# Per-token attention in score blocks of four tokens instead of eight, with its stages moved in the loop

## Chip, cores and metric

One core of a Trainium2 chip runs the whole program. The metric is the device time of one execution in microseconds (us). The kernel before takes 1196.86 us, the median of 3 runs (1196.32 to 1197.43).

## What is computed

The input is 8192 tokens of 256 features, in fp32 (4 sequences of 2048). A normalized copy passes a pre-norm transformer block whose attention runs inside each token, over its 16 heads; then a mixture of two chosen experts per sequence is added. The part that the change touches, in the reference:

```python
fq = jax.nn.elu(q) + 1.0
fk = jax.nn.elu(k) + 1.0
kv = jnp.einsum('bhnd,bhne->bnde', fk, v)
qkv = jnp.einsum('bhnd,bnde->bhne', fq, kv)
k_sum = fk.sum(axis=1)
qk = jnp.einsum('bhnd,bnd->bhn', fq, k_sum)
attn = qkv / (qk[..., None] + 1e-06)
```

The kernel uses the equivalent form per token n: the score of head h against head g is fq[h,n]·fk[g,n], the output of head h is the sum over g of score times v[g,n], and a column of ones beside v gives the denominator. The rest of the block (projections, an MLP of 1024 with exact gelu, layer norms, the experts) is the same before and after.

## The kernel before, in words

**Tiles and stages.** The tokens are cut into 16 tiles of 512. Each engine walks the same list of stages (`walk`, L134); `LAG` (L44) says how many iterations behind the newest tile a stage works, so one iteration of the loop (FULL, L46; HEAD, L48, at the start of a sequence) holds stages of up to six tiles. The list is written out by hand. Each engine issues its part of each stage in this order and waits on semaphores whose target values `walk` counts with the table `INC` (L70). An iteration has three sections here: the M stages (MLP of one tile, mixed with the attention of the tile behind it), the features and projections (X, VT, D2, A2, experts F1 and F3), and the ending (B0, H, FX, F2).

**Attention.** A tile's features q and k go through a DRAM scratch (`qk_dram`, stores L349 in stage D2, loads L372 in K0 and K1, 8 DMAs each), so that the 16 features of a head stand on 16 partitions, in four row groups (quarters j of the tile, 32 partitions apart). v goes the same way (`v_dram`, loads L361 in VL, 8 DMAs, then transposes in VT into `vb`). `scores(r)` (L913) takes 8 tokens times 16 heads as one 128 by 128 block: K is 16 rows, so four such matmuls, one for each quarter, can run in four row tiles of the array, each into its own bank of `ps`. A tile has 4 rounds of 4 blocks by 4 quarters, 16 matmuls a round; fp32 makes each matmul two records of the profile with a weight load each, 32 a round. Of a 128 by 128 block only the entries within a token count, one in eight; `masked(r)` (L675) multiplies by a 0/1 mask on VectorE, four banks of 512 columns a round, into `am` (two buffers). `weighted(r)` (L924) multiplies `am` (K 128) by v and ones (32 columns), four column tiles, into bank `pw[0]`, again 32 records a round; ScalarE copies it to `ot` (L532). After round 2 and round 4 SyncE stores half of `ot` to `nd_dram` (L377) and reads it back token by token (three loads, L382), in stages M2 and M4; VectorE divides in N0 and N (`divided`, L712).

**Stages M1 to M4 on TensorE** (L968 to L987), where `up` is one of the 8 up projections of the MLP (6 matmuls of 512 columns, L959) and `down` one of its 8 down projections (12 matmuls of 256 columns, L944):

- M1: up(0), up(1), scores(1), weighted(0), down(0)
- M2: up(2), scores(2), down(1), up(3), weighted(1), down(2)
- M3: up(4), scores(3), down(3), up(5), weighted(2), down(4)
- M4: up(6), down(5), up(7), weighted(3), down(6)

Before down(m) TensorE waits for VectorE's rest(m) (L694), which follows two gelus of ScalarE (L525, L526). scores(0) is B0, at the end of the iteration before, ahead of H: transposes of the second norm's output, from which ScalarE and VectorE make `hT` (L513, L710) that up(0) reads. F2 transposes the expert sum, adds it (L834) and stores the output (L400).

**SyncE's order** in an iteration: input load (L), x2 store (XS), 8 loads of v (VL), 8 of q and k for the first half (K0, after M1), nd store and 3 loads (M2), 8 loads (K1), nd store and 3 loads (M4), x2 load (XL), feature stores (D2), output store (F2). Each waits for its semaphores with all later DMAs queued behind it.

## Time and profile before

| | |
|---|---|
| median of 3 runs | 1196.86 us |
| profiled execution, its own time | 1194.7 us |
| its span in the trace | 1192.9 us |
| TensorE matmul busy | 1048.4 us (88%) |
| VectorE busy | 729.8 us (61%) |
| ScalarE busy | 499.5 us (42%) |
| GpSimd busy | 178.5 us (15%) |
| mean DMA share of queue 1 | 36.0% |
| granted TensorE clock, mean | 0.928 of full |

Busy is the union of an engine's instructions. The profiled execution took 1.8 us more than its span, and lies 2.2 us under the median. A granted clock of 1.0 is 2.4 GHz, of 0.5 is 1.2 GHz. M stages with attention of a tile run in iterations that begin (first up projection) at 117.5, 178.7, 240.4, 302.0, 363.6, 436.6, 500.6, 564.5, 630.3, 702.9, 766.9, 830.8, 896.1, 967.8 and 1032.5 us; one more tile's attention runs without an MLP between 61 and 90 us. The iterations from 436.6 on are preceded by F2. In section 3 of the page queue q1 carries SyncE's DMAs.

### The profile page before, as it was taken

The numbers are of one execution on the slowest core, as the hardware profiler recorded it, in microseconds if no ns is written. First come the engines' busy times: TensorE is split into PE (matmuls) and PEld (weight loads), VectorE is DVE, ScalarE is ACT, GpSimd is POOL, SyncE is SP. The second block draws the span as 40 slices with busy tenths as digits, with TensorE's granted clock in tenths as the row PEclk, the third lists the DMA queues.
The fourth block names the chain that finished last, engine by engine and source line by source line (L and its number), as shares of the span: only waits on it lengthen the run. The fifth ranks groups of instructions, "written<-read, shape, count | busy, mean of one in ns | idle before, by whom it ended". The sixth has DMA issues, their size and how long they took to land.

```text
span 1192.9 us, 23418 instructions
## 1 busy us (share of the span) xinstructions
PE 1048.4 (88%) x8136; PEld 779.5 (65%) x8136; DVE 729.8 (61%) x1692; ACT 499.5 (42%) x771; POOL 178.5 (15%) x113
## 2 busy tenths in 40 slices
PE   5767989898998899999999899999999896987856
PEld 3445858676777668585867667685868565665623
DVE  2286566666666666766666675766667674645333
ACT  2313444544353444445453545444453433332322
POOL 1021020211111111102021112112020111111000
PEclk9757989999898899999999999999999899998969
DMA  5635343434242443443544344433445434121023
GB/s 178 149 76 122 78 121 79 124 75 123 71 114 77 113 109 95 119 102 93 135 101 118 107 111 106 119 93 105 115 101 138 108 84 97 37 65 68 14 75 106
DMA packets 255833, 119.93 MB, mean 101 GB/s; under 512 B 225168, under 2 KB 241808, under 8 KB 255504
## 3 DMA queue, kind: packets, MB, share of 16 engines
q1 hardware_dynamic: 249104, 108.47, 36.0%
q10 hardware_dynamic: 6656, 10.50, 2.4%
q8 instruction: 45, 0.74, 0.3%
q14 instruction: 28, 0.23, 0.1%
HBM read 60.20 MB, written 58.72 MB: 100 GB/s over the span
## 4 chain that ended last, share of the span: by engine, by line
PE 72%; issue 11%; DVE 9%; POOL 2%; DMA 2%; ACT 2%; DVEq 0%; SPq 0%; ACTq 0%; POOLq 0%
PE pw L959 16%; PE pj L944 15%; PE ps L920 10%; PE ps L902 7%; PE pw L930 5%; PE pw L870 5%; PE pj L870 4%; PE pw L902 3%; DVE am L680 3%; PE ps L1001 3%; PE ps L858 2%; DVE hT L710 1%; POOL x_sb L447 1%; PE pw L910 1%; ACT hidden L526 1%
## 5 line engine op out<-in xcount | busy, mean ns | idle before, releaser
L959 PE MATMUL pw<-hT,w_fc 128*128 128x512 f32 x768 | 212.1, 417 | 30.4 <-DVE hT L710 29.7
L944 PE MATMUL pj<-w_pj,hidden 128*128 128x256 f32 x1536 | 214.1, 289 | 1.4 <-DVE hidden L694 1.4
L694 DVE TENSOR_TENSOR hidden<-xhT,hidden 128x512 fp32r<-128x512 f32 x128 | 88.6, 692 | 201.1 <-ACT hidden L526 201.1
L944 PEld LDWEIGHTS pj<-w_pj,hidden 128*128 128x128 f32 x1536 | 192.3, 189 | 22.5 <-issue 14.9
L525 ACT ACTIVATE xhT<-pw,col 128x512 f32<-128x512 f32 x128 | 88.1, 688 | 279.9 <-PE pw L959 279.3
L959 PEld LDWEIGHTS pw<-hT,w_fc 128*128 128x128 f32 x768 | 144.5, 199 | 66.1 <-DVE hT L710 31.7
L680 DVE TENSOR_TENSOR am<-ps,mask 128x512 f32<-128x512 f32 x256 | 158.9, 684 | 17.6 <-PE ps L920 17.5
L920 PE MATMUL ps<-kq 16*128 16x128 f32 x2048 | 146.9, 438 | 16.0 <-DVE am L680 9.2
L920 PEld LDWEIGHTS ps<-kq 16*128 16x128 f32 x2048 | 128.5, 329 | 42.3 <-issue 33.3
L902 PE MATMUL ps<-xhT,w_qkv 128*128 128x512 f32 x256 | 120.6, 627 | 2.5 <-ACT xhT L478 2.5
L532 ACT ACTIVATE ot<-pw,den_eps 128x512 f32<-128x512 f32 x64 | 81.8, 1278 | 49.6 <-PE pw L930 49.6
L719 DVE RECIPROCAL nd<-nd 128x256 f32<-128x256 f32 x32 | 56.0, 1749 | 60.2 <-DMA nd<-scratch_nd 60.2
L902 PEld LDWEIGHTS ps<-xhT,w_qkv 128*128 128x128 f32 x256 | 51.0, 205 | 61.6 <-issue 58.4
L526 ACT ACTIVATE hidden<-pw,col 128x512 fp32r<-128x512 f32 x128 | 87.2, 681 | 0.0
L672 DVE SCALAR_TENSOR_TENSOR fqk<-am 128x512 f32<-128x512 f32 x64 | 43.2, 690 | 59.6 <-ACT am L502 59.6
L444 POOL TENSOR_TENSOR x<-x,row 128x1024 f32<-128x1024 f32 x16 | 37.7, 2354 | 271.5 <-DVE x_sb L755 271.5
L1001 PE MATMUL ps<-w_o,hT 128*128 128x256 f32 x384 | 57.0, 308 | 21.2 <-DVE hT L730 21.2
L930 PE MATMUL pw<-am,vb 128*32 128x128 f32 x2048 | 73.0, 286 | 1.9 <-ACT ot L532 1.4
L930 PEld LDWEIGHTS pw<-am,vb 128*32 128x32 f32 x2048 | 54.6, 113 | 23.2 <-issue 16.4
L1001 PEld LDWEIGHTS ps<-w_o,hT 128*128 128x128 f32 x384 | 51.0, 203 | 28.7 <-DVE hT L730 21.6
L870 PE MATMUL pw<-zT,w_e 128*128 (+1 forms) x128 | 59.9, 612 | 7.2 <-DMA b_e<-in_eb 7.2
L902 PE MATMUL pw<-xhT,w_qkv 128*128 128x512 f32 x128 | 57.5, 592 | 0.0
(109 smaller groups left out, 1165.0 us busy)
## 6 DMA issues: line engine op xcount, KB each, us to landing
scratch_nd<-ot SPq DMA_DIRECT2D x32, 512.0 KB, 4.1
nd<-scratch_nd SPq DMA_DIRECT2D x96, 128.0 KB, 2.6
x_sb<-in_x SPq DMA_DIRECT2D x16, 512.0 KB, 4.6
scratch_v<-feat_v ACTq DMA_DIRECT2D x16, 512.0 KB, 2.8
scratch_q<-fqk SPq DMA_DIRECT2D x32, 256.0 KB, 2.7
scratch_k<-fqk SPq DMA_DIRECT2D x32, 256.0 KB, 3.0
vd<-scratch_v SPq DMA_DIRECT2D x128, 64.0 KB, 2.7
kq<-scratch_q SPq DMA_DIRECT2D x128, 64.0 KB, 2.5
```

The source lines that it names most:

```text
L525: nc.scalar.activation(gelub[:, m % 2], pw[n], ACT.Gelu, bias=b_fc[:, m:m + 1])
L526: nc.scalar.activation(hidden[:, m % SLOTS, 0], pw[n], ACT.Gelu, bias=b_fc[:, m:m + 1]).then_inc(S[f"pw_free{n}"], 1)
L532: nc.scalar.activation(dst[:, r // 2, RG * (r % 2):RG * (r % 2 + 1)], src, ACT.Identity, bias=den_eps[:, :]).then_inc(S["pw_free0"], 1)
L680: last = nc.vector.tensor_tensor(am[:, r % 2, j].rearrange("p (g n) -> p g n", n=P), ps[:, j].rearrange("p (g n) -> p g n", n=P), mask[:, ...
L694: nc.vector.tensor_tensor(hidden[:, m % SLOTS, 1], gelub[:, u], hidden[:, m % SLOTS, 0].bitcast(f32), ALU.subtract).then_inc(S["rest_ready ...
L870: last = nc.tensor.matmul(bank, w[:, c, P * m:P * (m + 1)], zT[:, p.t % RING, c], start=(c == 0), stop=(c == NC - 1))
L902: last = nc.tensor.matmul(bank, w_qkv[:, j // NC, c, P * (j % NC):P * (j % NC + 1)], xhT[:, c], start=(c == 0), stop=(c == NC - 1))
L920: last = nc.tensor.matmul(ps[:, j, P * g:P * (g + 1)], kd[rows, r // 2, at_g], qd[rows, r // 2, at_g], start=True, stop=True)
L930: last = nc.tensor.matmul(pw[0][32 * j:32 * j + 32, P * g:P * (g + 1)], vb[:, GG * j + RG * r + g], am[:, r % 2, j, P * g:P * (g + 1)], st ...
L944: last = nc.tensor.matmul(pj[u][:, D * s:D * (s + 1)], hidden[:, m % SLOTS, a, lo:lo + P], w_pj[:, b, m], start=(m == 0 and n == 0 and s = ...
L959: last = nc.tensor.matmul(pw[bank], w_fc[:, b, c, P * m:P * (m + 1)], hT[:, a, c], start=(n == 0), stop=(n == len(order) - 1))
L1001: last = nc.tensor.matmul(sa[u][:, D * s:D * (s + 1)], attnT[:, a, c, lo:lo + P], w_o[:, b, c], start=(c == 0 and n == 0), stop=(c == NC - ...
```

## The change

Blocks are of 4 tokens by 16 heads, 64 by 64. Two of them (v, which splits each half of a quarter once more) stand in the upper and lower 64 columns of the array, so `scores` issues eight tile positions in turn (4 row groups, 2 column groups) and fills all four banks of `ps` in one call for half of the tile. There are now two calls, scores(0) in B0 and scores(1) in M2, each of 64 matmuls (128 records), and two of `weighted` with 64 matmuls (128 records; K 64, 32 columns of weights, 64 columns moved; 2 row groups by 4 column groups), which write banks sa[0] and sa[1] (banks 0 and 1 of `ps`) instead of pw[0]. VectorE masks 4 banks a call, 8 instructions a tile instead of 16, and `am` is one buffer. ScalarE still copies 4 banks a tile into `ot`, two after each `weighted`. With `pw[0]` free, the up projections alternate between pw[0] and pw[1]. TensorE's order becomes:

- M1: up(0), up(1), weighted(0), down(0)
- M2: up(2), scores(1), down(1), up(3), down(2)
- M3: up(4), down(3), weighted(1), up(5), down(4)
- M4: up(6), down(5), up(7), down(6)

In the stage list K0 stands before M1 and K1 behind M2, N0 stands before M4 instead of behind it, and H before B0. Scratch q and k are stored in runs of 32 tokens (128 bytes) instead of 64; v is loaded with 16 DMAs instead of 8, in the same short runs; M2 and M4 wait for sa instead of pw[0] before the nd store.

```diff
-TB = 4
+TB = 2
 TA = 2 * TB
...
+BLOCK = TA * H
+KG = HALF // (2 * TA)
+ROUNDS = 4
...
-FULL = ["L", "XS", "VL", "M1", "K0", "J2", "Y", "M2", "DS", "M3", "Z", "D1", "K1", "M4", "N0", "XL", "X", "J7", "JA", "YB", "E", "VT", "N", "D2", "A2",
-        "F1", "R", "F3", "F4", "SA", "B0", "H", "FX", "F2"]
+FULL = ["L", "XS", "VL", "K0", "M1", "J2", "Y", "M2", "K1", "DS", "M3", "Z", "D1", "N0", "M4", "XL", "X", "J7", "JA", "YB", "E", "VT", "N", "D2", "A2",
+        "F1", "R", "F3", "F4", "SA", "H", "B0", "FX", "F2"]
...
-    "kq_in0": {"K0": 32 * NQ}, "kq_in1": {"K1": 32 * NQ}, "v_in": {"VL": 32 * NQ},
+    "kq_in0": {"K0": 32 * NQ}, "kq_in1": {"K1": 32 * NQ}, "v_in": {"VL": 64 * NQ},
...
-        am = sb("am", [P, 2, NQ, 512])
+        am = sb("am", [P, NQ, 512])
...
-        qk_dram = [nc.dram_tensor(f"scratch_{n}", (2, 2 * NQ, D, HALF), f32, kind="Internal").ap() for n in "qk"]
+        qk_dram = [nc.dram_tensor(f"scratch_{n}", (2, 4 * NQ, D, HALF // 2), f32, kind="Internal").ap() for n in "qk"]
...
                         for b in range(2):
-                            sp.dma_start(vd[2 * j + b::2 * NQ].rearrange("p (h t) -> p h t", h=H), src[j, b]).then_inc(S["v_in"], 16)
+                            for v in range(2):
+                                sp.dma_start(vd[2 * j + b::2 * NQ].rearrange("p (v h t) -> p v h t", v=2, h=H)[:, v],
+                                             src[j, b, v]).then_inc(S["v_in"], 16)
...
-                    wait("pw_free0", at("pw_free0", 1))
+                    for u in range(2):
+                        wait(f"sa_free{u}", at(f"sa_free{u}"))
                     sp.dma_start(nd_dram.rearrange("j e h t -> (j e) h t")[:, :, part], ot[:, :, part]).then_inc(S["nd_out"], 16)
...
+                        if "B" in parts and r % 2 == 0 and u == int(r == 0):
+                            dst = ot[:, :, :].rearrange("p h (b v a k) -> p b v k h a", b=2, v=2, k=KG)
+                            for v in range(2):
+                                wait(f"sa_full{v}", at(f"sa_full{v}", 1))
+                                src = sa[v].rearrange("p (k h a) -> p k h a", k=KG, h=H)
+                                nc.scalar.activation(dst[:, r // 2, v], src, ACT.Identity,
+                                                     bias=den_eps[:, :]).then_inc(S[f"sa_free{v}"], 1)
...
-                def scores(r):
+                def scores(b):
 
                     wait("sc_free", at("sc_free"))
-                    for g in range(RG):
-                        at_g = slice(RG * (r % 2) + g, P * HG, HG)
-                        for j in range(NQ):
-                            rows = slice(32 * j, 32 * j + HD)
-                            last = nc.tensor.matmul(ps[:, j, P * g:P * (g + 1)], kd[rows, r // 2, at_g], qd[rows, r // 2, at_g],
-                                                    start=True, stop=True)
+                    for k in range(KG):
+                        for v in range(2):
+                            for j in range(NQ):
+                                rows = slice(32 * j, 32 * j + HD)
+                                cols = slice(BLOCK * KG * v + k, BLOCK * KG * (v + 1), KG)
+                                last = nc.tensor.matmul(ps[BLOCK * v:BLOCK * (v + 1), j, BLOCK * k:BLOCK * (k + 1)],
+                                                        kd[rows, b, cols], qd[rows, b, cols], start=True, stop=True)
                     last.then_inc(S["sc_full"], 1)
 
-                def weighted(r):
+                def weighted(b):
 
                     wait("sc_free", at("sc_free"))
...
+                    for k in range(KG):
+                        for v in range(2):
+                            rows = slice(BLOCK * v, BLOCK * (v + 1))
+                            cols = slice(BLOCK * k, BLOCK * (k + 1))
+                            for j in range(NQ):
+                                last = nc.tensor.matmul(sa[v][32 * j:32 * j + 32, cols], vb[rows, KG * (2 * j + b) + k],
+                                                        am[rows, j, cols], start=True, stop=True)
```

## Rows read from the trace of the kernel before

**Rows 1.** The page: span, TensorE's busy time, the chain that ended last by line

```profile
span 1192.9 us, 23418 instructions
...
PE 1048.4 (88%) x8136; PEld 779.5 (65%) x8136; DVE 729.8 (61%) x1692; ACT 499.5 (42%) x771; POOL 178.5 (15%) x113
...
PE pw L959 16%; PE pj L944 15%; PE ps L920 10%; PE ps L902 7%; PE pw L930 5%; PE pw L870 5%; PE pj L870 4%; PE pw L902 3%; DVE am L680 3%; PE ps L1001 3%; PE ps L858 2%; DVE hT L710 1%; POOL x_sb L447 1%; PE pw L910 1%; ACT hidden L526 1%
```

**Rows 2.** Groups by line, shapes apart: busy us, mean ns of one, idle before

```profile
L920 PE MATMUL ps<-kq 16*128 16x128 f32 x2048 | 146.9, 438 | 16.0 <-DVE am L680 9.2 <-DVE x L740 6.8
...
L680 DVE TENSOR_TENSOR am<-ps,mask 128x512 f32<-128x512 f32 x256 | 158.9, 684 | 17.6 <-PE ps L920 17.5
...
L532 ACT ACTIVATE ot<-pw,den_eps 128x512 f32<-128x512 f32 x64 | 81.8, 1278 | 49.6 <-PE pw L930 49.6
...
L719 DVE RECIPROCAL nd<-nd 128x256 f32<-128x256 f32 x32 | 56.0, 1749 | 60.2 <-DMA nd<-scratch_nd 60.2
```

**Rows 3.** TensorE in time, inner iteration at 564: start, us, idle before

```profile
564.52 4.60 PE L959 MATMUL pw<-hT,w_fc 128*128 128x512 f32 x12 [2.16 <-DVE hT L710]
...
569.05 2.29 PE L920 MATMUL ps<-kq 16*128 16x128 f32 x32
...
571.28 1.08 PE L930 MATMUL pw<-am,vb 128*32 128x128 f32 x32
...
572.29 1.67 PE L944 MATMUL pj<-w_pj,hidden 128*128 128x256 f32 x12
...
597.99 1.70 PE L944 MATMUL pj<-w_pj,hidden 128*128 128x256 f32 x12
```

**Rows 4.** Weight loads in time, the first 0.3 us of the weighted sums at 571

```profile
571.28 0.38 PEld L930 LDWEIGHTS pw<-am,vb 128*32 128x32 f32 x16 [0.22 <-issue]
```

**Rows 5.** TensorE and VectorE in time, end of that iteration

```profile
623.65 2.29 PE L920 MATMUL ps<-kq 16*128 16x128 f32 x32
...
625.87 1.09 PE L858 MATMUL pw<-ident,hn 128*128 128x128 f32 x8
...
628.41 1.28 DVE L710 TENSOR_TENSOR hT<-pw,hT 128x512 fp32r<-128x512 f32 x2
...
629.61 1.28 DVE L834 TENSOR_TENSOR out_sb<-pj,out_sb 128x512 f32<-128x512 f32 x2
...
630.32 1.89 PE L959 MATMUL pw<-hT,w_fc 128*128 128x512 f32 x7 [2.49 <-DVE hT L710]
```

**Rows 6.** SyncE's queue in time, same iteration (start, us of issuing)

```profile
565.58 0.38 SPq L400 DMA_DIRECT2D out<-out_sb  x1
...
568.75 5.29 SPq L361 DMA_DIRECT2D vd<-scratch_v  x8
...
574.77 1.92 SPq L372 DMA_DIRECT2D kq<-scratch_q  x4
...
583.29 0.57 SPq L377 DMA_DIRECT2D scratch_nd<-ot  x1
...
587.46 1.50 SPq L382 DMA_DIRECT2D nd<-scratch_nd  x3
```

**Rows 7.** The page, DMA issues: KB each, us to landing

```profile
nd<-scratch_nd SPq DMA_DIRECT2D x96, 128.0 KB, 2.6
```

**Rows 8.** Windows around one score burst each: busy, granted clock, DMA share

```profile
70.80:73.10 2.30, 2.27 (x36) 2.05 (x39) 0.00 (x0) 0.00 (x0) 0.00 (x0) 0.50 0.00 0
...
569.00:571.30 2.30, 2.30 (x37) 2.03 (x36) 1.16 (x2) 1.27 (x2) 0.00 (x0) 1.00 0.91 301
```

**Rows 9.** TensorE in time, end of an iteration without expert stages

```profile
165.56 3.44 PE L1001 MATMUL ps<-w_o,hT 128*128 128x256 f32 x24
...
178.69 4.80 PE L959 MATMUL pw<-hT,w_fc 128*128 128x512 f32 x12 [1.80 <-DVE hT L710]
```

**Rows 10.** TensorE in time, last iteration with attention

```profile
1032.53 3.07 PE L959 MATMUL pw<-hT,w_fc 128*128 128x512 f32 x12 [1.91 <-DVE hT L710]
...
1079.31 5.03 PE L1001 MATMUL ps<-w_o,hT 128*128 128x256 f32 x24 [10.97 <-DVE hT L730]
```

More of the change, by code:

```diff
@@ L26 @@
 HALF = QT // 2
-TB = 4
+TB = 2
 TA = 2 * TB
-GG = QT // TA
-RG = 4
-HG = GG // 2
-ROUNDS = GG // RG
+BLOCK = TA * H
+KG = HALF // (2 * TA)
+ROUNDS = 4
 TERMS = ((0, 0), (1, 0), (0, 1))
@@ L515, in run @@
                     parts, r = of_round(p.stage)
-                    if "C" in parts:
-                        for m in (2 * r, 2 * r + 1):
-                            n = int(m != 1)
-                            more = int(r > 0 and m % 2)
-                            wait(f"pw_full{n}", at(f"pw_full{n}", more + 1))
+                    for u in range(2):
+                        if "C" in parts:
+                            m = 2 * r + u
+                            wait(f"pw_full{u}", at(f"pw_full{u}", 1))
@@ L949, in up @@
                 def up(m):
-                    bank = int(m != 1)
-                    wait(f"pw_free{bank}", at(f"pw_free{bank}", int(m > 1 and m % 2)))
+                    bank = m % 2
+                    wait(f"pw_free{bank}", at(f"pw_free{bank}"))
                     if m == 0:
                         wait("h_round", at("h_round"))
-                        wait("pw_free0", at("pw_free0"))
+                        for c in range(NC):
+                            wait(f"pw_free{c}", at(f"pw_free{c}"))
                     order = [(a, b, c) for a, cb in ((0, (0, 1)), (1, (0,))) for c in range(NC) for b in cb]
```

110 lines of the change are left out of this document (48 added, 62 removed), and 2 rows, old and new, of the table INC.

## The prediction

> **What bounds the kernel now.** I read the page first: TensorE is busy for 1048 of 1193 us, and the chain that ended last runs mainly over its lines, 10% of it scores and 5% weighted sums [rows 1]. Then the groups: a score record takes part in 146.9 us of work, and the masks cost VectorE 158.9 us, but VectorE isn't the bound, so halving its 256 masks is worth nothing by itself beyond what TensorE waits for [rows 2]. The timeline of one iteration shows TensorE without a gap through the M stages; what it loses lies at the ending, where up(0) waits 2.2 to 2.5 us for hT, which VectorE makes behind four masks [rows 3, 5]. Last I read SyncE's queue, which this change loads further [rows 6]: there the price of the change hides.
>
> A word on names: E is the end of the experts' F3 (623.65, where B0 begins), T0 the start of up(0), and F2 end the end of the output addition (L834). S is one of the new score calls and W one of the new weighted calls, each half a tile, each 128 records.
>
> **Price of S.** Now 32 records go by in 2.23 us (569.05 to 571.28), eight groups of four row tiles, 0.28 us a group [rows 3]. This pace is the same at a granted clock of 0.50 and of 1.00 [rows 8], so it is set by how four row tiles read 128 columns, not by the array's clock. Lower end: a group of eight tiles with half the columns takes half the time, 16 x 0.14 = 2.2 us. Upper end: a group takes as long as now, since it reads as many columns in all, 16 x 0.28 = 4.5 us. I take 2.4, near the lower end, because a row group and its columns are what seems to set the pace.
>
> **Price of W.** Now 32 records take 1.01 us, 31.6 ns each, with 128 columns moved in four column tiles [rows 3]. Lower end: half the columns, eight tiles, 16 x 0.063 = 1.0 us. Upper end: the pace per record stays, 128 x 31.6 ns = 4.0 us. Of the 32 weight loads at 571.28 the first 16 start within 0.38 us [rows 4], less than 24 ns apart, and about 18 when the last one's own duration is taken off. At 18 ns a record, W = 2.3 us, which I take; S at that pace would be 2.3 as well.
>
> A page of the Trainium skill, "TensorE: Matmul & The Clock Gate" (Part 1), gives a floor of about 25 ns from one matmul's start to the next, however few columns. By it S = W = 3.2 us. The loads in rows 4 start closer than that, but a short burst is no proof for 128 in a row, so it stands among the rivals.
>
> **M stages, TensorE alone.** Before, T0 to down(6) is 33.5 us in the iteration at 564 [rows 3], of which 3 score rounds and 4 weighted rounds are 3 x 2.23 + 4 x 1.01 = 10.7, and 1.5 come from up(0) and up(1) at a low clock (4.6 us against 3.1, [rows 3, 10]). The rest is 21.3. After: 21.3 + S + 2W = 28.3, plus some 0.5 in M3, where gelu(5) stands behind two copies into ot of 1.28 us each [rows 2] and down(5) comes too early for it.
>
> **Ending.** Before: B0, then H (0.93 us to the next start), F2 as much, then the wait; T0 is at E + 6.7 [rows 5]. After: H first, so ScalarE and VectorE make hT (1.1 + 1.3 us) while S runs, and that wait is gone: T0 at E + 1.9 + S = E + 4.3. VectorE's masks come behind hT (2.48 us) and F2's addition behind these: F2 end at E + 1.0 + S + 0.1 + 2.4 + 1.2 = E + 7.1, where it was E + 7.2. So up(0) starts 2.8 us before F2 end instead of 0.9 after. W(0) needs the masks only after two up projections, 3.1 us; they are hidden.
>
> **What is late next: SyncE.** Its iteration begins at F2 end, with the output store. The 8 loads of v start 3.3 us later and take 5.3 us, 0.66 each; K0's 8 loads start at 574.77 and take 3.8; nd store to first nd load is 4.2 us [rows 6]; the third load is issued 1.0 later and lands after 2.6 [rows 7]. Now 16 v loads stand there: 3.3 + 10.6 (5.6 x 2 = 11.2 over all 16 bursts) + 0.7 + 3.8 + 0.5 + 4.2 + 3.6 = F2 end + 27.3. Until then N0 can't divide. Before, N0 stood behind M4 and found its data there; now it stands before M4, and VectorE's rest(6), for which down(6) waits, is queued behind it. N0 takes 1.75 for the reciprocal [rows 2], 0.8 for two products, rest(6) 0.7: down(6) at F2 end + 30.6. TensorE alone would want it at 28.3 - 2.8 = F2 end + 25.5. So it **waits 5 us** in each iteration that follows an F2, and what the smaller blocks gained in M is mostly idle time there. An idle stretch of this kind costs the clock too: after 10.97 us of idle the output projection took 5.03 us, otherwise 3.44 [rows 9, 10]. I add 1.5 us.
>
> **The sum.** Eight iterations with F2 before them (436.6 to 896.1): F2 end to down(6) was 31.8 us in the mean (30.8 to 33.3 by the timeline; 32.6 in rows 3 and 5) and becomes 30.6, -1.2; the ending -0.1; clock +1.5: together +0.2 each, +2. Five without (117.5 to 363.6): their v loads don't wait for F2 but begin before T0, so N0 finds its data. M: S + 2W + 0.5 - 10.7 = -3.2; ending: from the end of H to T0 there were 1.8 us of idle [rows 9] and now stands S, +0.6; -2.6 each, -13. The last one (1032.5) has no loads of v, q and k at all: before, TensorE stood idle for 10.97 us until the division was done, 46.8 us after T0 [rows 10]. Now W(1) ends at T0 + 20.7 (six up, four down projections, S and 2W), copies 2.6, store to landing 7.8, division and split 4.6: T0 + 35.7, -11, and T0 itself 2.3 earlier: -13. The one before it (967.8) has the same gap, but SyncE's loads before the second store: about -4. The tile without an MLP (61 to 117): its second store no longer waits for a fourth round, about -2. Edits with no price: the masks saved (VectorE had time), the alternating up banks (gelus end before the bank's next use), runs of 128 bytes (more packets, in a queue busy 36% of the time; its cover would go if the q and k stores lasted into K0, 15 us later).
>
> Sum -30 on the profiled 1194.7, which lies 2.2 under the median: **1166 us**.
>
> **Rivals.**
> 1. *N0's data come in time.* If v loads of half the bytes are issued in half the time, SyncE is 5.3 us sooner and the wait vanishes, and with it the cold clock: eight times -6.6 more, about 1113. For: they carry half. Against: K0's loads, of the same 64 KB but in far fewer pieces, take 0.48 each [rows 6], so pieces seem to count rather than bytes, and their number stays.
> 2. *A floor between.* A long run of records settles at 25 ns each, halfway between the 18 of rows 4 and the 31.6 of rows 3: S = W = 3.2. Then the five cost 9.6 - 10.7 + 1.4 = +0.3 each, the eight +0.8, the last two -13, the first tile -1: about 1190. The page named above would have this.
> 3. *The pace per record stays* (the one on the slower side). TensorE starts a weight load and matmul no faster than 31.6 ns in a long run: S = W = 4.0. Then the five cost 12.1 - 10.7 + 2.2 = +3.6 each, the eight +0.3, the last two -9: +11, **1208**. It decides from 28 ns a record on. For it: no row shows more than 32 records in a row. Against: rows 4.
> 4. *All eight tiles share a reader*, S = 4.5, W = 2.3: the five +1.1 each, the eight +1.9, the last two -11: +10, about 1207. For it: the pace of rows 8 doesn't follow the clock. Against: if a column group has its own reader, it is the row groups that share one, and each column group reads half.
>
> **Chances.** Forecast 0.47, rival 1 0.13, rival 2 0.12, rival 3 0.12, rival 4 0.12, other 0.04. The range reaches from rival 1 to rival 3, 1112 to 1208. Within 0.2% (2.4 us, about what a measurement of this kernel can tell from no change) only an accident between the cases would lie. Faster 0.72, same 0.04, slower 0.24. The cases of the faster side alone lie between 1112 and 1190.
>
> **What would show it.** Score bursts of 128 records in 2.4 us, and weighted ones in 2.3; no wait of up(0) for hT; a new wait of VectorE's first reciprocal for nd, and of down(6) for rest(6), some 5 us in ten iterations; v loads of 0.66 us each in SyncE's queue. Wrong would be: bursts over 3.5 us; no wait at N0; a wait of H for hn that grows because B0 no longer covers it.

## The result, and the profile after

The changed kernel takes **1215.7 us** (median of four runs, 1209.9 to 1216.9) against 1196.6 for the kernel before on the same chip: ratio 1.0149, 95% interval [1.0116, 1.0181]. It is slower by 1.5%, and the interval excludes no change. The forecast was 1166 us, with the range up to 1208. The profiled execution has a span of 1213.9 us.

The page of the changed kernel, parts 1, 3, 4 and 5 (L939 is down, L955 up, L911 scores, L924 weighted sums, L679 the masks, L693 rest, L709 the division's reciprocal):

```profile
span 1213.9 us, 31449 instructions
...
PE 1004.7 (83%) x12232; PEld 763.5 (63%) x12232; DVE 688.2 (57%) x1564; ACT 488.7 (40%) x771; POOL 185.5 (15%) x113
...
q8 instruction: 101, 1.65, 0.6%
...
PE 54%; issue 15%; DVE 12%; SPq 8%; DMA 4%; ACT 3%; POOL 2%; DVEq 1%; ACTq 0%; POOLq 0%
...
L939 PE MATMUL pj<-w_pj,hidden 128*128 128x256 f32 x1536 | 228.2, 302 | 49.5 <-DVE hidden L693 48.7
...
L955 PE MATMUL pw<-hT,w_fc 128*128 128x512 f32 x768 | 228.4, 442 | 17.2 <-issue 17.0
...
L679 DVE TENSOR_TENSOR am<-ps,mask 128x512 f32<-128x512 f32 x128 | 79.5, 684 | 28.4 <-PE ps L911 28.4
...
L911 PE MATMUL ps<-kq 16*64 16x64 f32 x4096 | 81.6, 312 | 5.4 <-issue 3.3
...
L709 DVE RECIPROCAL nd<-nd 128x256 f32<-128x256 f32 x32 | 55.9, 1748 | 16.5 <-DMA nd<-scratch_nd 16.5
...
L924 PE MATMUL ps<-am,vb 64*32 64x64 f32 x4096 | 51.4, 232 | 16.6 <-DVE am L679 10.3
```

TensorE is busy for 44 us less than before (1048.4 in [rows 1]), scores for 81.6 instead of 146.9 and masks for 79.5 instead of 158.9 [rows 2]. So the work did shrink; the time went into waits, of which two are new. Down waits 48.7 us for rest (1.4 us before). Up waits 17.0 us for "issue", that is for nothing that the profile shows, where it waited for hT. New too is that the queue that brings instructions carries 101 packets, 1.65 MB; the page of before has 45 and 0.74 MB.

TensorE in time, the changed kernel, the M stages of the iteration at 568 and its end (start, us):

```profile
568.09 5.01 PE L955 MATMUL pw<-hT,w_fc 128*128 128x512 f32 x12 [3.92 <-issue]
573.03 1.47 PE L924 MATMUL ps<-am,vb 64*32 64x64 f32 x126
575.58 0.30 PE L924 MATMUL ps<-am,vb 64*32 64x64 f32 x2 [1.09 <-issue]
...
590.82 1.48 PE L924 MATMUL ps<-am,vb 64*32 64x64 f32 x128
...
597.98 1.56 PE L955 MATMUL pw<-hT,w_fc 128*128 128x512 f32 x6
602.13 2.15 PE L939 MATMUL pj<-w_pj,hidden 128*128 128x256 f32 x12 [2.59 <-DVE hidden L693]
604.08 1.91 PE L848 MATMUL ps<-ident,xhat 128*128 128x128 f32 x8
...
630.25 2.42 PE L911 MATMUL ps<-kq 16*64 16x64 f32 x128
633.72 1.91 PE L1043 MATMUL pj<-ident,acc 128*128 128x128 f32 x8 [1.06 <-issue]
638.60 2.92 PE L955 MATMUL pw<-hT,w_fc 128*128 128x512 f32 x6 [2.97 <-issue]
```

S is 2.4 us, as forecast. W is 1.5, not 2.3. But from E (629.4, the end of F3) to T0 (638.6) it is 9.2 us, and this holds idle stretches that wait for no other engine. Around down(6), the same kernel, VectorE (its first row from an earlier iteration) and SyncE's queue in time:

```profile
457.05 1.75 DVE L709 RECIPROCAL nd<-nd 128x256 f32<-128x256 f32 x1 [1.41 <-DMA nd<-scratch_nd]
...
597.38 1.38 DVE L617 TENSOR_SCALAR xhat<-x_sb,mv,rs 128x256 f32 x4
...
598.66 1.75 DVE L709 RECIPROCAL nd<-nd 128x256 f32<-128x256 f32 x1
...
600.45 0.76 DVE L712 TENSOR_TENSOR nd<-nd 128x256 f32<-128x256 f32 x2
601.38 1.29 DVE L693 TENSOR_TENSOR hidden<-xhT,hidden 128x512 fp32r<-128x512 f32 x2 [0.17 <-DVE nd L712]
```

```profile
565.90 0.37 SPq L402 DMA_DIRECT2D out<-out_sb  x1
...
569.05 12.55 SPq L361 DMA_DIRECT2D vd<-scratch_v  x16
582.33 2.98 SPq L373 DMA_DIRECT2D kq<-scratch_q  x4
...
587.59 0.58 SPq L379 DMA_DIRECT2D scratch_nd<-ot  x1
591.77 2.51 SPq L384 DMA_DIRECT2D nd<-scratch_nd  x3
```

The reciprocal starts where D1's xhat ends (598.7), without an idle stretch ahead of it: what holds rest(6) up in this iteration is VectorE's own program, Z, D1, N0 in a row, and not late data. In the five iterations without an F2 before them and in four of the eight with one it is the same, and down(6) waits 1.2 to 2.6 us. In the other four of the eight (T0 at 426.9, 638.6, 711.4 and 922.2) and in the one behind them (997.3) the first half's reciprocal does wait for nd, 1.4 to 1.9 us and once 5.7, as the first row shows, and down(6) waits 4.0 to 6.9 us. That is 11.7 us of late data in all ahead of N0. The last lines show the queue that the forecast had made the cause: 12.55 us for 16 loads, 0.78 each.

Windows of the changed kernel around that wait (us, PE busy, PEld, DVE, ACT, POOL, granted clock, DMA share, GB/s):

```profile
592.00:598.00 6.00, 6.00 (x66) 5.38 (x54) 2.52 (x7) 4.42 (x6) 1.09 (x1) 1.00 0.47 118
598.00:602.00 4.00, 1.54 (x8) 0.92 (x6) 3.79 (x8) 1.29 (x3) 0.00 (x0) 1.00 0.73 160
602.00:606.00 4.00, 3.87 (x21) 3.87 (x22) 0.68 (x2) 0.60 (x1) 0.00 (x0) 0.64 0.42 92
```

The granted clock is 1.00 up to 602 and 0.64, between its levels of 0.5 and 1.0, in the 4 us behind the 2.6 us of idle; down(6) takes 2.15 us where the down projections at 593.73 and 596.55 take 1.6. So the wait is paid twice.

I cut the eight iterations that follow an output addition (T0 at 436.6 to 896.1 before, 426.9 to 922.2 after) into stretches, each a mean over eight, from the first and last rows of these bursts in the timeline:

| | E to T0 | F2 end to down(6) | down(6) to next E | period | first four periods |
|---|---|---|---|---|---|
| before | 6.3 | 31.7 | 27.6 | 66.4 | 61.5 |
| changed | 7.9 | 34.7 | 29.5 | 71.3 | 60.0 |
| changed, forecast | 4.3 | 30.6 | as before, clock +1.5 | 66.6 | 58.9 |

E to F2 end is 7.0 us in nearly all of them, as forecast (7.1), so the period is the sum of this and the next two stretches. The eight cost 39 us more than before, where the forecast had 2; the five periods that end by 426.9 gained 9, where it had 13.

### The profile page after: what moved, and what is told of

It is laid out like the page before. It is cut to its first block, busy times and chain, and to the rows that moved or that the text cites. A ratio compares the mean times of both kernels' runs of the same rounds, so it can differ in the third digit from the quotient of the medians.

```text
span 1213.9 us, 31449 instructions
## 1 busy us (share of the span) xinstructions
PE 1004.7 (83%) x12232; PEld 763.5 (63%) x12232; DVE 688.2 (57%) x1564; ACT 488.7 (40%) x771; POOL 185.5 (15%) x113
## 3 DMA queue, kind: packets, MB, share of 16 engines
q8 instruction: 101, 1.65, 0.6%
## 4 chain that ended last, share of the span: by engine, by line
PE 54%; issue 15%; DVE 12%; SPq 8%; DMA 4%; ACT 3%; POOL 2%; DVEq 1%; ACTq 0%; POOLq 0%
PE pj L939 10%; PE pw L955 8%; PE ps L892 7%; PE ps L911 5%; SPq L361 5%; PE pw L860 4%; PE pj L860 4%; PE pw L892 3%; PE ps L999 3%; PE ps L848 3%; DVE nd L709 2%; PE ps L924 2%; DMA scratch_nd<-ot 2%; SPq L373 2%; PE pw L848 2%
## 5 line engine op out<-in xcount | busy, mean ns | idle before, releaser
L939 PE MATMUL pj<-w_pj,hidden 128*128 128x256 f32 x1536 | 228.2, 302 | 49.5 <-DVE hidden L693 48.7
L939 PEld LDWEIGHTS pj<-w_pj,hidden 128*128 128x128 f32 x1536 | 213.7, 206 | 66.2 <-DVE hidden L693 55.1
L955 PE MATMUL pw<-hT,w_fc 128*128 128x512 f32 x768 | 228.4, 442 | 17.2 <-issue 17.0
L693 DVE TENSOR_TENSOR hidden<-xhT,hidden 128x512 fp32r<-128x512 f32 x128 | 87.4, 692 | 203.6 <-ACT hidden L525 201.0
L955 PEld LDWEIGHTS pw<-hT,w_fc 128*128 128x128 f32 x768 | 157.3, 217 | 52.7 <-issue 20.0
L679 DVE TENSOR_TENSOR am<-ps,mask 128x512 f32<-128x512 f32 x128 | 79.5, 684 | 28.4 <-PE ps L911 28.4
L532 ACT ACTIVATE ot<-ps,den_eps 128x512 f32<-128x512 f32 x64 | 70.2, 1189 | 46.0 <-PE ps L924 45.7
L911 PE MATMUL ps<-kq 16*64 16x64 f32 x4096 | 81.6, 312 | 5.4 <-issue 3.3
L911 PEld LDWEIGHTS ps<-kq 16*64 16x64 f32 x4096 | 74.3, 209 | 16.4 <-issue 14.1
L440 POOL TENSOR_TENSOR rs<-var,mhalf 128x8 f32 (+1 forms) x16 | 30.4, 1898 | 230.3 <-DVE var L632 224.8
L709 DVE RECIPROCAL nd<-nd 128x256 f32<-128x256 f32 x32 | 55.9, 1748 | 16.5 <-DMA nd<-scratch_nd 16.5
L924 PE MATMUL ps<-am,vb 64*32 64x64 f32 x4096 | 51.4, 232 | 16.6 <-DVE am L679 10.3
L745 DVE TENSOR_TENSOR x_sb<-pj,x_sb 128x512 f32<-128x512 f32 x32 | 20.6, 686 | 74.5 <-PE pj L939 74.5
```

The lines of the kernel that those rows point to most:

```text
L679: last = nc.vector.tensor_tensor(am[:, j].rearrange("p (k n) -> p k n", n=BLOCK), ps[:, j].rearrange("p (k n) -> p k n", n=BLOCK), mask[:, ...
L693: nc.vector.tensor_tensor(hidden[:, m % SLOTS, 1], gelub[:, u], hidden[:, m % SLOTS, 0].bitcast(f32), ALU.subtract).then_inc(S["rest_ready ...
L709: link(nc.vector.reciprocal(d, d))
L911: last = nc.tensor.matmul(ps[BLOCK * v:BLOCK * (v + 1), j, BLOCK * k:BLOCK * (k + 1)], kd[rows, b, cols], qd[rows, b, cols], start=True, s ...
L924: last = nc.tensor.matmul(sa[v][32 * j:32 * j + 32, cols], vb[rows, KG * (2 * j + b) + k], am[rows, j, cols], start=True, stop=True)
L939: last = nc.tensor.matmul(pj[u][:, D * s:D * (s + 1)], hidden[:, m % SLOTS, a, lo:lo + P], w_pj[:, b, m], start=(m == 0 and n == 0 and s = ...
```

## The experiments

Each was timed beside the kernel before on the same chip, which took 1195.5 us there for the first four rows of this table, 1198.9 for the next four, then 1197.1 (four), 1196.7 (four) and 1196.4 (two); so the ratios are the numbers to compare.

| run | us | ratio [95%] | instruction packets |
|---|---|---|---|
| pad512 | 1198.7 | 1.0025 [1.001, 1.004] | 49 |
| pad256 | 1196.6 | 1.0012 [0.9994, 1.003] | 47 |
| n0_back | 1158.9 | 0.9695 [0.9671, 0.9719] | 101 |
| w_half | 1176.6 | 0.9847 [0.9813, 0.9881] | 55 |
| n0_w_half | 1127.0 | 0.9406 [0.9382, 0.9429] | 55 |
| n0_vl_late | 1185.0 | 0.989 [0.985, 0.993] | 101 |
| h_first | 1175.5 | 0.9812 [0.9787, 0.9837] | 45 |
| sc64 | 1146.2 | 0.9572 [0.9548, 0.9596] | 54 |
| n0_ahead | 1196.0 | 0.9993 [0.9976, 1.0009] | 45 |
| n0_wait_only | 1162.8 | 0.9713 [0.9689, 0.9738] | 101 |
| sc64_pad2 | 1155.1 | 0.9644 [0.9619, 0.9669] | 59 |
| sc64_pad5 | 1497.5 | 1.2501 [1.2467, 1.2535] | 64 |
| n0_shift | 1145.0 | 0.9565 [0.9512, 0.9617] | 64 |
| n0_shift_256 | 1186.7 | 0.9923 [0.9893, 0.9954] | 102 |
| after_shift | 1197.7 | 1.0015 [0.9998, 1.0033] | 64 |
| n0_shift_kq | 1122.8 | 0.9404 [0.9355, 0.9453] | 64 |
| kq_only | 1148.0 | 0.9601 [0.9581, 0.962] | 101 |
| best | 1119.6 | 0.9351 [0.9328, 0.9374] | 65 |

### N0's place

**n0_back**, the changed kernel with one stage put back (here and below, an order of stages is cut to its part that changes, and stands so in FULL and HEAD):

```
-  "Z", "D1", "N0", "M4",
+  "Z", "D1", "M4", "N0",
```

> The changed kernel with stage N0 behind M4 again, as before the change. Down(6) then doesn't wait for the reciprocal and products (2.6 us in an iteration by the trace of the changed kernel). Theory A: that is 2 to 3 us in up to 13 iterations, 1175 to 1200, and the waits at the loop's end stay. Theory B (this is the whole loss against the forecast): 1150 to 1170, with no idle time of TensorE left over 2 us in an iteration.

The move alone is worth 57 us (54 by the ratios). The time is theory B's, but not all of its picture: idle stretches of about 3.5 us at the loop's end stay, as theory A said. In the profile of n0_back (groups):

```profile
L939 PE MATMUL pj<-w_pj,hidden 128*128 128x256 f32 x1536 | 213.1, 289 | 4.5 <-DVE hidden L693 3.4 <-issue 0.6
```

Down's wait for rest falls from 48.7 to 3.4 us and down's own time by 15. TensorE's busy time is 979.3 instead of 1004.7, 25 us less with the same records, and its idle gaps over 0.4 us sum to 168.6 instead of 200.0, 31 less: nearly half of the price was slower work and not waiting. Down's 15 and the transposes of xhat right behind down(6) (25.7 us busy against 19.4) make up most of these 25 us, which fits the lower clock in the windows above. What remains of the change gains 3%.

**n0_wait_only** tells late data from VectorE's own work. It leaves out the first half's division and keeps the wait for its data (the count of `dve_chain` follows, not shown):

```
 if p.stage == "N0":
-    divided(0)
+    wait("num_in0", at("num_in0"))
```

> Leaves out: the first half's division (a reciprocal and two products in each of 16 tiles); the wait for its data stays in its place ahead of M4. One edit to the changed kernel. Theory A (N0's own work is what down(6) waits for): near the kernel with N0 behind M4, 1150 to 1170 us. Rival B (the wait for the data is what costs, as forecast): over 1195 us.

1162.8 us, ratio 0.9713, within 4 us of n0_back: theory A's range. Its groups:

```profile
L939 PE MATMUL pj<-w_pj,hidden 128*128 128x256 f32 x1536 | 216.4, 292 | 17.7 <-DVE hidden L693 16.9 <-issue 0.2
...
L709 DVE RECIPROCAL nd<-nd 128x256 f32<-128x256 f32 x16 | 28.0, 1749 | 34.9 <-DMA nd<-scratch_nd 34.9
```

A wait for data is left (16.9 us before down, where n0_back has 3.4), of which only 2 to 4 us show in the time. So in this kernel, with everything else as it is, N0's 2.5 us of VectorE work in each tile were most of the price. Two limits: the run also spares VectorE that work elsewhere, and it says nothing of a kernel in which TensorE comes sooner; after_shift below is one, and there the data are late.

**n0_ahead**, the same move in the kernel before:

```
-  "Z", "D1", "K1", "M4", "N0",
+  "Z", "D1", "K1", "N0", "M4",
```

> The kernel before with one edit: N0 ahead of M4, where the changed kernel has it. Theory A (N0's place costs its own work on VectorE, 1.75 us and two products of 0.4 each, between D1 and rest(6), wherever its data are): down(6) waits some 2 to 4 us in each of 13 iterations, 1215 to 1245 us. Rival B (only late data cost, as the forecast had it): K1 is still ahead of the division's loads in SyncE's queue, so the loads of nd land at about the same time as in the changed kernel and the wait comes only behind an output addition: 8 x 3 to 5 us, and none in the five iterations without one. Rival C (what N0's move cost in the changed kernel came from its meeting with the shorter stages alone): within 0.3% of before.

0.9993: no cost at all. Both A and B fall, C stands. VectorE and then TensorE of n0_ahead in time show why:

```profile
592.92 0.69 DVE L694 TENSOR_TENSOR hidden<-xhT,hidden 128x512 fp32r<-128x512 f32 x1 [1.92 <-ACT hidden L526]
...
598.83 0.69 DVE L694 TENSOR_TENSOR hidden<-xhT,hidden 128x512 fp32r<-128x512 f32 x1 [0.17 <-DVE nd L722]
```

```profile
591.40 1.08 PE L930 MATMUL pw<-am,vb 128*32 128x128 f32 x32
...
598.56 1.08 PE L930 MATMUL pw<-am,vb 128*32 128x128 f32 x32
599.58 1.69 PE L944 MATMUL pj<-w_pj,hidden 128*128 128x256 f32 x12
```

From the start of rest(5) to the end of rest(6), with Z, D1 and N0 between them, VectorE takes 6.6 us here (592.92 to 599.52) and 6.6 in the changed kernel (595.48 to 602.1). But here TensorE does two weighted rounds of 1.0 us between up(5) and down(6), and rest(6) is done 0.06 us before down(6) starts. The changed kernel has no block work there: TensorE stood ready at 599.5, 2.6 us too soon. The data were there too: no first half waits for nd in these stages. N0 cost nothing as long as TensorE had something else to do.

### The fetching of TensorE's instructions

A second part of the time hangs on the 101 packets. At 1.65 MB for 101 a packet is 16 KB. If an instruction takes 64 bytes, that is a piece of 256. Two counts bear it out: n0_shift_256 below has 256 instructions more than n0_back, run once, and one packet more; and the 24464 weight loads and matmuls of the changed kernel alone fill 96 such pieces, so its 101 packets are about what a kernel needs that fetches everything each time. Before, 16272 fill 64, and 45 packets came. I counted TensorE's instructions in the inner loop's body (one for each record of a weight load and of a matmul, each wait and each increment): 1177 before, 1684 after, 1434 in sc64. The first trials:

**pad512**, **pad256**: the kernel before with 512 or 256 such instructions in the inner loop, in the branch of FX that is never taken.

```
 with pe.If(more > 0):
     ...
+    for n in range(PAD):
+        expert(pj[0][:, :], w_e[:, 0], 0)
```

> The kernel before, with 64 expert products (512 instructions of TensorE, weight loads and matmuls) put into the branch of stage FX that is never taken, in the inner loop's copy alone; the loop body has then about 1690 instructions of TensorE instead of 1177, as long as that of the changed kernel (1684), and executes what it did. Theory A (instruction fetch: the changed kernel's inner loop no longer stays on the chip, and each turn of it waits for its instructions): q8 'instruction' packets rise from 45 to over 70, the branch back at the loop's end takes some us, and the time rises by 15 to 35 us, to 1212 to 1232. Theory B (the loss is SyncE's chain and the earlier N0 alone): 1197 within 2 us.

> As pad512 with 32 products (256 instructions), a body of 1433. The changed kernel's loop without expert stages has 1582 and shows no fetch from its second turn on. Theory A with a limit between 1582 and 1684: as before, 1197 within 2 us, q8 near 45. Theory A without a limit (each instruction more costs): half of pad512's loss. Theory B: 1197.

Within 0.25%, and 4 and 2 packets more: theory A's 15 to 35 us for pad512 did not come. Code that is jumped over is not fetched on each turn, so these runs don't test what they were made for: they say only that skipped code costs next to nothing.

**w_half** and **n0_w_half** (the second with N0 behind M4) make the executed body shorter, 1428. They leave out every second block of the weighted sums (the place of the last increment follows, not shown):

```
-  for k in range(KG):
+  for k in range(0, KG, 2):
```

> The changed kernel that leaves out every second block of the weighted sums (half of them; 256 instructions fewer, body of 1428). Work left out on TensorE: 2 x 0.74 us a tile, 24 us in all at most. Theory A: the fetches of the inner loop go as well, q8 back to about 50, 5 us an inner iteration less on top: 1150 to 1175. Theory B: only what was left out, and most of that is given back as waiting at down(6): 1195 to 1216.

> Leaves out: every second block of the weighted sums. Two edits together: N0 behind M4 again, and half of the weighted blocks left out, so that the loop body of TensorE has some 256 instructions fewer (about 1430 where the body before had 1180 and the changed one 1680). Theory A (instruction fetch: a body that is too long for TensorE's instruction store is fetched anew on every turn, which costs waits at the loop's end and inside the stages): beyond the work left out, at most 16 x 1.5 = 24 us, another 20 to 40 us go, so 1095 to 1118 us; the instruction queue has some 50 packets instead of 101, and no loop branch over 1 us. Rival B (fetching costs nothing on the path; the eight iterations are slow because of SyncE's chain of loads): at least 1158.9 - 24 = 1135 us.

Both have 55 packets. w_half, at 1176.6 us, is 2 us above theory A's range and far below B's. n0_w_half lies between its theories, 32 us under n0_back; the half of the weighted sums left out is worth 16 x 2 x 0.75 = 24 us at the W of 1.5 that I measured, so 8 us or more are something else, less than theory A's 20. The trace says why: in four of its turns that follow another turn of the loop, F2 end to down(6) is 22.8 to 23.1 us (32.7 to 34.3 in n0_back's), but down(6) to next E is 31.4 instead of 25.7. The gain runs into a wait for the division's data, to which I come back.

**sc64_pad5** and its control **sc64_pad2** make it longer with nothing but increments between the matmuls of up:

```
 start=(n == 0), stop=(n == len(order) - 1))
+if n < len(order) - 1:
+    for _ in range(PAD + (PAD + n) // 5):
+        pe.sem_inc(held, 1)
```

> sc64 with 12 increments of a semaphore that nobody waits for, executed by TensorE's sequencer between the matmuls of each up projection: 96 instructions more in the loop body, 1530 in all, no work for the array. The control for sc64_pad5. Both theories: within 0.5% of sc64 (1146.2 us), no more instruction packets than its 54, no new loop branch over 1 us.

> sc64 with 30 such increments in each up projection, 240 more in the loop body, 1674 in all, as long as the changed kernel's (1684). Theory A (a body beyond a limit between 1582 and 1684 instructions is fetched anew on every turn): some 100 instruction packets instead of 54, loop branches of 4 us, up(0) late by 4 us and the M stages longer by some 4 us in eight or nine iterations: 1190 to 1225 us. Rival B (the length costs nothing; what delays the changed kernel is its order of stages or its bursts of 128 records): no more than 1% above sc64, 1158 us, and 54 packets.

sc64_pad2 is 0.8% above sc64 and has 59 packets, a little more than said. sc64_pad5 is a miss for both theories: 1497 us, yet only 64 packets and up(0) on time. The array simply waited for the increments: up(0) and up(1) took 9.9 us instead of 3.1. The useful result is that a body of 1674 instructions, 10 fewer than the changed kernel's, is not fetched anew. Length alone is not it. By my count that body begins 33 instructions into a piece and touches 7 pieces; the changed kernel's begins 202 into one and touches 8.

**n0_shift**, **n0_shift_256** and **after_shift** move the body and change nothing else in it: 108 (256, 108) increments, executed once at the very start.

```
 def _(pe):
     wait = waiter(pe)
+    for _ in range(108):
+        pe.sem_inc(held, 1)
```

> The kernel with N0's move alone (n0_back, 1158.9 us) and 108 increments of a semaphore that nobody waits for, executed once by TensorE's sequencer at the very start: the inner loop's body, 1684 instructions, begins 54 instead of 202 instructions into a piece of 256, and so touches 7 pieces instead of 8. Theory A (what is fetched anew is a body that touches more than 7 pieces): about 60 instruction packets instead of 101, no loop branches of 4 us in the inner loop's turns, and some 5 us less in each of its 5 turns that follow another: 1125 to 1142 us. Rival B (length decides, or something else than position): 101 packets and 1155 to 1163 us.

> The control for n0_shift: 256 such increments instead of 108, so that the body begins where it did within a piece (202) and again touches 8. Theory A: 102 packets, loop branches of 4 us, 1155 to 1170 us (the increments themselves may delay the start by up to some us). Rival B (the increments at the start help in themselves, whatever their number): as n0_shift.

> The changed kernel with the same 108 increments at the start. Theory A: the repeated fetching goes, and with it what it costs beside N0's place: 1215.7 less 20 to 35 us, so 1180 to 1196 us, about as fast as the kernel before. Rival B: within 0.3% of the changed kernel, 1212 to 1219 us.

Position decides. The pages of n0_shift, n0_shift_256 and after_shift, in this order:

```profile
q8 instruction: 64, 1.05, 0.4%
```

```profile
q8 instruction: 102, 1.67, 0.6%
```

```profile
q8 instruction: 64, 1.05, 0.4%
```

TensorE in time at the end of a turn that follows another, first n0_back, then n0_shift:

```profile
479.93 4.83 PE L955 MATMUL pw<-hT,w_fc 128*128 128x512 f32 x12 [3.46 <-issue]
485.21 1.02 PE L924 MATMUL ps<-am,vb 64*32 64x64 f32 x71 [0.45 <-issue]
```

```profile
478.75 2.21 PE L913 MATMUL ps<-kq 16*64 16x64 f32 x120
481.86 1.09 PE L1045 MATMUL pj<-ident,acc 128*128 128x128 f32 x8 [0.90 <-issue]
482.79 3.06 PE L957 MATMUL pw<-hT,w_fc 128*128 128x512 f32 x12
```

With the body in 7 pieces the 3.5 us at the loop's end are gone, and up(0) and up(1) take 3.1 us at a granted clock of 1.00 instead of 4.8 at 0.62. The increments cost at the start: the first T0 is 127.3 with 108 and 148.3 with 256, instead of 117.0, about 0.1 us each. As timed, all three lie above theory A's ranges, by 3, 17 and 2 us. Less these 10 and 31 us at the start they take 1135, 1155 and 1187 us, against 1158.9, 1158.9 and 1215.7 without: -24, -3 and -28. Counted in the profiles from the first T0 to the end, which needs no such deduction, it is -20.1, 0.0 and -26.5. So **the repeated fetching costs the changed kernel 26 to 28 us**, and the page of the kernel before, with its shorter body, shows none of it.

The same trace holds a second finding. In after_shift, SyncE's queue, VectorE and TensorE in time, the iteration whose F2 ends at 508.0:

```profile
511.32 10.46 SPq L361 DMA_DIRECT2D vd<-scratch_v  x16
...
535.36 1.75 DVE L709 RECIPROCAL nd<-nd 128x256 f32<-128x256 f32 x1 [2.92 <-DMA nd<-scratch_nd]
...
538.83 2.93 PE L941 MATMUL pj<-w_pj,hidden 128*128 128x256 f32 x12 [5.61 <-DVE hidden L693]
```

The v loads take 0.65 us each, the data come at F2 end + 27.4, and down(6) waits 5.6 us and comes at F2 end + 30.9. This is the forecast's wait (27.3, 5 and 30.6). Over the eight such iterations down(6) waits 2.7 to 6.8 us, 5.1 in the mean. In the changed kernel TensorE and VectorE are so late from fetching that half of these iterations find their data.

### What is late next: SyncE's loads

**n0_vl_late**: in n0_back the loads of v moved behind M2.

```
-  "L", "XS", "VL", "K0", "M1", "J2", "Y", "M2", "K1",
+  "L", "XS", "K0", "M1", "J2", "Y", "M2", "VL", "K1",
```

> N0 behind M4 again, and the 16 loads of v moved in SyncE's program behind stage M2, so that the loads of q and k for scores(1) no longer stand behind them. Theory A (instruction fetch sets the rest of the price): 1150 to 1165 us, within 0.6% of the kernel with N0's move alone (1158.9). Rival B (SyncE's chain still sets down(6) or the last wait in the eight iterations behind an output addition): 15 us or more are gained, under 1144 us. Rival C (v, loaded later, is now what weighted(0) waits for): slower than 1170 us.

Slower than n0_back by 2%, rival C's figure (8 of the 26 us are there before the first T0, at 125.2 instead of 117.0); but the reciprocal's wait for nd grew from 28.7 to 75.7 us. So it wasn't weighted(0) that waited, but the division's second half, whose store and loads now stood behind 16 loads of v.

**n0_shift_kq** takes the 16 loads of q and k from ahead of the division's store and loads, **kq_only** does so with the body at its old position, **best** with 80 increments where TensorE waits for the second tile's xhat.

```
-  "VL", "K0", "M1", "J2", "Y", "M2", "K1", "DS", "M3", "Z", "D1", "M4", "N0",
+  "VL", "M1", "J2", "Y", "M2", "DS", "M3", "Z", "D1", "M4", "K0", "K1", "N0",
```

> n0_shift with SyncE's loads of q and k (K0 and K1, 8 each) behind M4, so that both stores and loads for the division come 4 to 9 us sooner after the loads of v. Theory A (with the fetching gone, N's second half waits for its data, and the loads of q and k ahead of them are why): 4 to 6 us less in each of the iterations behind an output addition, n0_shift less 25 to 45 us, 1085 to 1115 us. Rival B (the wait moves to first scores, for which q and k now come too late, or the data were not late): no more than 5 us less than n0_shift, or slower.

> n0_shift_kq without its increments: N0 and the loads of q and k behind M4, and the loop's body at its old position (8 pieces). Theory A (with the body fetched anew on each turn, TensorE is late enough that the division's data are there; their order is worth something only once that is gone): 1150 to 1160 us, within 1% of n0_back's 1158.9, and 101 packets. Rival B (the order of the loads is worth its 22 us by itself): 1130 to 1142 us.

> n0_shift_kq with 80 increments instead of 108, executed once where TensorE waits 7.3 us for the second tile's xhat before the loop: the body begins 26 instructions into a piece and touches 7. Theory A: first up(0) near 117 us, some 64 packets, 9 us less than n0_shift_kq's 1122.8: 1108 to 1118 us. Rival B (the margin of 26 is too small, and the body is fetched anew): 101 packets, as kq_only.

The division's row in the groups of n0_shift and of n0_shift_kq:

```profile
L709 DVE RECIPROCAL nd<-nd 128x256 f32<-128x256 f32 x32 | 55.9, 1748 | 60.0 <-DMA nd<-scratch_nd 60.0
```

```profile
L709 DVE RECIPROCAL nd<-nd 128x256 f32<-128x256 f32 x32 | 55.8, 1744 | 1.0 <-DMA nd<-scratch_nd 1.0
```

59 us of waiting vanish and 22 us of time (29 between the two profiles), less than theory A's 25 to 45; the rest was idle time of VectorE that cost nothing. In kq_only the same edit gives 11 us, between its theories: half of it needs the fetching gone. The means of the same stretches:

| | E to T0 | F2 end to down(6) | down(6) to next E | period |
|---|---|---|---|---|
| n0_back | 8.0 | 30.9 | 28.1 | 66.0 |
| after_shift | 5.8 | 31.8 | 29.5 | 68.2 |
| n0_shift | 5.7 | 25.7 | 31.1 | 63.7 |
| n0_shift_kq | 5.7 | 26.0 | 27.6 | 60.7 |
| h_first | 4.3 | 29.6 | 27.6 | 64.1 |
| sc64 | 4.3 | 27.5 | 28.8 | 62.6 |

Read down the columns: N0 and the fetching both sit in the second, and once they are out of it the wait shows up in the third.

**best** has the lowest time, 1119.6 us, 6.5% under the kernel before and 7.9% under the changed one, and 2 us above its theory's range; its interval overlaps that of n0_shift_kq. Its first T0 is back at 116.5, 10 us earlier than in n0_shift_kq, but at most 3 us of that are left at the end: its up(0) and up(1) take 4.0 to 4.6 us in turns where n0_shift_kq has some at 3.1. Why its clock is lower there (0.905 in the mean against 0.918) stays open.

### The parts that paid

**h_first**: the kernel before, H ahead of the first scores.

```
-  "SA", "B0", "H", "FX", "F2"
+  "SA", "H", "B0", "FX", "F2"
```

> The kernel before with one edit: transposes for hT ahead of the first scores at the end of an iteration. Theory A (the wait for hT of 2.2 to 2.5 us was real time of the path, and the masks behind it are hidden by up(0) and up(1)): 13 iterations x 2 us = 26 us less at most, 1168 to 1185 us. Rival B (the wait only moves, since the output addition stands later on VectorE and SyncE's chain begins with it): within 0.3% of 1195.5 us.

-1.9%, Theory A: E to T0 is 4.3 in the mean (3.9 in seven of eight), and F2 end is E + 6.9, where it was E + 7.2.

**sc64**: h_first with the new scores alone, in four rounds; the weighted sums stay in 128-row tiles, and the mask zeroes the two quadrants that a 64 by 64 block leaves.

```
+for v in range(2):
+    at_g = slice(512 * v + RG * (r % 2) + g, 512 * (v + 1), HG)
+    for j in range(NQ):
+        at_v = ps[64 * v:64 * (v + 1), j, P * g:P * (g + 1)].rearrange("p (h v a) -> p v h a", v=2, a=TB)[:, v]
+        last = nc.tensor.matmul(at_v, kd[rows, r // 2, at_g], qd[rows, r // 2, at_g], start=True, stop=True)
```

> The kernel before, with its four rounds, its order of loads, its N0 and its weighted sums kept, but with score blocks of 64 by 64 in eight tiles (16 instead of 8 loads of v, in pieces of half the length; the mask zeroes the other two quadrants), and H ahead of B0. TensorE's loop body stays near 1430 instructions. Theory A: a score round falls from 2.23 us to 1.2, so four rounds in each of 14 tiles give 4 x 1.0 x 14 = 56 us where TensorE is the bound, and what H gives on top: 1125 to 1150 us. Rival B (SyncE's longer chain of v loads takes the place): 1165 to 1185 us. Rival C (a body of 1430 instructions is already fetched anew): long loop branches, over 1175 us.

1146.2 us, inside Theory A's range and 29 under h_first, where its sum had 56 for the scores: a round takes 1.4 us instead of the 1.2 put there, and the reciprocal's wait for nd is 70.7 us (61.8 in h_first). It beats the changed kernel by 5.7% without touching N0 or the weighted sums. Its scores take 88.1 us in all:

```profile
L924 PE MATMUL ps<-kq 16*64 16x64 f32 x4096 | 88.1, 316 | 10.1 <-DVE am L682 10.1
```

## Why the prediction was wrong

**Right: S, E to F2 end, and the wait for nd.** S was put at 2.4 and is 2.4. F2 end was put at E + 7.1 and is E + 7.0. The wait that the forecast made of SyncE's chain, "Until then N0 can't divide", is there with its size once the fetching is gone: in four turns of after_shift the data come at F2 end + 26.6 to 27.4 and down(6) at + 30.1 to 30.9, against 27.3 and 30.6 forecast. (The forecast's terms as written out, with 10.6 for the v loads, add up to 26.7; 27.3 takes the 11.2 in its bracket.) N0's place cost 5.3 us in each of the eight iterations (71.3 against 66.0), where 6.6 were forecast.

**Failed: "T0 at E + 4.3".** That sum holds in h_first (3.9) and nearly in n0_shift (5.0 to 5.3 in five of eight turns), but the changed kernel has 9.1 to 9.6 in five of eight turns, and its M stages are held up as well. What stood in its place is fetching, 26 to 28 us in all, in no term and no rival. The forecast counted the records of S and W and never asked how many instructions the loop holds; the queue of instructions stood on the page of before with 45 packets, and the chain had no row that hinted at it.

**Failed: "so N0 finds its data"**, which counted nothing for the five iterations without an F2. The data are there, but N0's own 2.5 us of VectorE work stand behind Z and D1 and ahead of rest(6) all the same. The first four periods are 61.5 before, 60.0 after and 57.4 in n0_back: N0's place costs 2.6 in each, and without it the change gains 4.1, which is the forecast's 2.6 and the 1.6 of W. The same blindness is in the rivals: all asked when data come, none what VectorE does in the 3 us before rest(6), though rows 2 gave the reciprocal's 1.75. The forecast even added it behind the data; it was missing where the data were early.

**Mis-sized: W**, 2.3 in the forecast, 1.5 to 1.6 in the trace, 128 records at 12 ns. The value was taken from the first 16 loads of a burst [rows 4]; the lower end, half the columns and twice the tiles, was nearer (1.0). This erred against the change, by 1.6 us a tile, and counts only where the stages go at TensorE's pace: in the five iterations it does, and where down(6) waits for nd it drops out. From T0 to down(6) TensorE alone was put at 28.3; in four of the eight iterations of n0_shift it takes 25.7 to 25.8; 1.6 of the difference is W and the rest open. The Trainium skill, "TensorE: Matmul & The Clock Gate" (Part 1), has a floor of about 25 ns from one matmul's start to the next. The 12 ns a record here, and 19 in the score bursts, lie under it, so rivals 2 and 3 fall, and rival 4 with S. Two records make one matmul of the program, so counted in those it is 23 and 38 ns, and only the weighted sums lie under the floor.

**Not weighed enough: the last iterations.** From T0 of the iteration at 967.8 (997.3 after) to the end 8 us were gained, where 17 were forecast. In the first of them the reciprocal waits 5.7 us for nd and down(6) 6.9, and the iteration takes 0.5 us more than before instead of 4 less. **N's own data** were not looked at either: with N0 put back, the loads of q and k ahead of the division's cost n0_back 11 us and n0_shift 22. That pieces count rather than bytes, as the argument against rival 1 said, is right: a v load of half the size takes 0.65 us in four of after_shift's eight iterations, against 0.66 [rows 6]. In the changed kernel's eight they take 0.72 to 0.89; four of these fall to 0.65 or 0.66 when the fetching goes, the others stay at 0.74 to 0.78, which no run explains.

**The sum**, by stretches of the two profiles: the forecast's span was 1162.9 (1192.9 - 30), the measured one is 1213.9, 51 us more.

| stretch | forecast | measured | off by |
|---|---|---|---|
| to the first T0 | -2 | -0.5 | +1.5 |
| five iterations without F2 | -13 | -9.2 | +4 |
| eight iterations behind F2 | +2 | +39.1 | +37 |
| from the iteration at 967.8 to the end | -17 | -8.4 | +9 |

In the five, N0's work adds 13 and W takes off 8. In the eight, 25 of the 37 are fetching (periods of 71.3 against 68.2 in after_shift); the other 12, 1.5 an iteration, stand in after_shift too, and no run isolates them: they stay open. The last line is in part the 5.7 us above.

## What to carry over

Before a stage is moved ahead of a projection, add up everything that its engine then does before the operation that the projection waits for, its arithmetic first and its data second, and ask what block work covers it now; the same move was free in one kernel and cost 57 us in the other. Do so for the iterations where the data are early as well. When the number of small matmuls in a loop doubles, look at the instruction queue's packets in the profile: if they rise with every turn, the body no longer stays where it is, and 80 instructions executed once before the loop can bring it back. Having mended one wait, read the next one's releaser before the next edit: a wait that a slower part hides, as fetching hid the one for nd here, shows only then.

## What was not expected of the hardware

- TensorE fetches a loop's body anew on each turn when it lies badly: 101 packets of 16 KB against 64 for the same body moved by 108 instructions, and 3 to 4 us at the loop's end; from E to down(6) n0_back takes 9 to 10 us longer than n0_shift in four of its turns. Bodies that by my count touch 7 pieces of 256 instructions stay (n0_shift, best, sc64_pad5), those that touch 8 don't (n0_back, n0_shift_256). The pieces' bounds are counted from the program, and that what is kept is 7 pieces is inferred, not shown.
- An increment of a semaphore on TensorE's queue costs some 0.1 us (10.3 us for 108). Two or three between matmuls nearly hide (12 in each of 128 up projections: 9 us in all); six between two matmuls don't (30 in each: 351 us).
- Eight array tiles with weights of 64 rows by 32 columns take a record every 12 ns for 128 in a row, with weights of 16 rows by 64 columns every 19 ns. At a granted clock of 0.50 the first take 2.0 us a burst instead of 1.5 (71.6 and 80.8 in the changed kernel), the second 2.4 as at 1.00 (75.7).
- Behind a gap of 2.6 us the granted clock was 0.64 in the next 4 us (602 to 606, the changed kernel).
- Two products of the division took 0.76 us at one place and 3.57 at another in one iteration of n0_shift_kq (511.02 and 515.32, VectorE in time):

```profile
511.02 0.76 DVE L712 TENSOR_TENSOR nd<-nd 128x256 f32<-128x256 f32 x2
...
515.32 3.57 DVE L712 TENSOR_TENSOR nd<-nd 128x256 f32<-128x256 f32 x2
```

Of the 32 such pairs in this trace, the 11 that overlap with GpSimd's work take 3.6 us and the 21 others 0.76; no run takes GpSimd's work away, so the cause is only argued.
